# Integer intermediates, a fused product-and-maximum pass and PSUM-resident tiles in the feed-forward block of a Perceiver kernel

## What is computed

```python
def act_qdq(x):
    qmax = 2.0 ** (ACT_BITS - 1) - 1.0                  # 32767
    scale = jnp.maximum(jnp.max(jnp.abs(x)) / qmax, 1e-12)
    return jnp.clip(jnp.round(x / scale), -qmax - 1.0, qmax) * scale
def fixed_qdq_u16(x):
    scale = 1.0 / 65536.0
    return jnp.clip(jnp.round(x / scale), 0.0, 65535.0) * scale
x = act_qdq(x)
up = act_qdq(x @ lpbq_dequant(w_up).T)
gate = act_qdq(x @ lpbq_dequant(w_gate).T)
sig = fixed_qdq_u16(jax.nn.sigmoid(gate))
gate = act_qdq(gate * sig)
o = act_qdq(gate * up)
return o @ lpbq_dequant(w_down).T
```

## Time and profile before

| | us |
|---|---|
| Median of 3 runs (lowest, highest) | 1110.4 (1108.04, 1111.61) |
| Profiled execution, its own time | 1106.35 |
| Its span, first to last instruction | 1104.6 |
| TensorE busy in the span | 1025.6 (93%) |
| VectorE busy | 821.7 (74%) |
| ScalarE busy | 495.0 (45%) |
| GpSimd busy | 405.3 (37%) |

### The profile page before, as it was taken

The page is one execution under the profiler, slowest core; times in us unless marked ns, Lnnn a source line. Parts: engine busy times, 40 slices in busy tenths (PEclk is TensorE's granted clock), DMA queues, the critical chain, the costliest instruction groups (busy, mean ns, idle before and its releaser), DMA issues.

```text
span 1104.6 us, 14650 instructions
## 1 busy us (share of the span) xinstructions
PE 1025.6 (93%) x4907; PEld 481.3 (44%) x4907; DVE 821.7 (74%) x1186; ACT 495.0 (45%) x739; POOL 405.3 (37%) x218
## 2 busy tenths in 40 slices
PE   7999999999999989999839999999988889888997
PEld 3444444444444444544314444444452234465453
DVE  5566666799999558585974479999957777476897
ACT  2255555566666627415774211101036725356164
POOL 4287787400000363100002086776426740084003
PEclk9999999999999999999959999999999999999999
DMA  6146454623434056402010235435310020000001
GB/s 233 66 154 192 157 183 161 218 95 111 170 142 144 17 211 247 173 3 94 1 44 33 98 136 211 177 154 210 80 39 1 1 79 1 1 2 1 2 1 39
DMA packets 41831, 112.65 MB, mean 102 GB/s; under 512 B 4512, under 2 KB 15296, under 8 KB 35648
## 3 DMA queue, kind: packets, MB, share of 16 engines
q1 hardware_dynamic: 38592, 101.13, 26.1%
q10 hardware_dynamic: 2880, 9.96, 2.7%
q0 software_dynamic: 320, 1.05, 0.3%
HBM read 103.18 MB, written 7.34 MB: 100 GB/s over the span
## 4 chain that ended last, share of the span: by engine, by line
PE 69%; DVE 18%; ACT 5%; issue 3%; DMA 3%; POOL 1%; DVEq 0%; SPq 0%; ACTq 0%; POOLq 0%
PE PS L767 5%; PE PS L768 5%; PE PS L769 5%; PE PS L798 5%; PE PS L800 5%; PE PS L799 5%; PE PS L1709 5%; PE PS L1711 5%; PE PS L1710 5%; PE PS L249 3%; PE PS L251 3%; PE PS L250 3%; DVE arena L2087 2%; DMA arena<-in_w 2%; DVE arena L1632 2%
## 5 line engine op out<-in xcount | busy, mean ns | idle before, releaser
L798 PE MATMUL PS<-arena 128*128 128x512 f16 x256 | 97.0, 379 | 2.4 <-DVE arena L689 1.3
L767 PE MATMUL PS<-arena 128*128 128x512 f16 x256 | 97.0, 379 | 2.0 <-DVE arena L616 2.0
L1709 PE MATMUL PS<-arena 128*128 128x512 f16 x256 | 97.0, 379 | 1.8 <-DVE arena L1555 1.8
L768 PE MATMUL PS<-arena 128*128 128x512 f16 x256 | 97.0, 379 | 0.0
L769 PE MATMUL PS<-arena 128*128 128x512 f16 x256 | 97.0, 379 | 0.0
L1710 PE MATMUL PS<-arena 128*128 128x512 f16 x256 | 97.0, 379 | 0.0
L1711 PE MATMUL PS<-arena 128*128 128x512 f16 x256 | 97.0, 379 | 0.0
L800 PE MATMUL PS<-arena 128*128 128x512 f16 x256 | 97.0, 379 | 0.0
L799 PE MATMUL PS<-arena 128*128 128x512 f16 x256 | 97.0, 379 | 0.0
L623 DVE TENSOR_TENSOR arena<-PS,arena 128x512 f32<-128x512 f32 x64 | 43.6, 681 | 58.0 <-ACT arena L547 58.0
L481 POOL TENSOR_TENSOR arena<-arena 128x2048 f16<-128x2048 f32 x16 | 66.0, 4127 | 38.4 <-ACT arena L540 38.1
(11 more groups left out here) (381 smaller groups left out, 2437.1 us busy)
## 6 DMA issues: line engine op xcount, KB each, us to landing
arena<-in_ctxT SPq DMA_DIRECT2D x32, 1024.0 KB, 6.2
arena<-in_ctx SPq DMA_DIRECT2D x16, 1024.0 KB, 5.3
arena<-in_w ACTq DMA_DIRECT2D x8, 1024.0 KB, 5.4
arena<-in_w SPq DMA_DIRECT2D x8, 1024.0 KB, 6.6
XN<-in_ffnGU SPq DMA_DIRECT2D x16, 384.0 KB, 3.4
XN<-in_WinT SPq DMA_DIRECT2D x16, 290.0 KB, 5.0
gu_hi<-arena SPq DMA_DIRECT2D x16, 192.0 KB, 3.5
gu_lo<-arena SPq DMA_DIRECT2D x16, 192.0 KB, 3.4
```

The costliest lines, as they stand in the source:

```text
L767: pe.matmul(bank, CHI[:, b, e, cols], QHI[:, e, :], start=(e == 0), stop=False)
L768: pe.matmul(bank, CHI[:, b, e, cols], QLO[:, e, :], start=False, stop=False)
L798: pe.matmul(PS[:, t, :], PHI[:, j, cols], CHI[:, b, j, :], start=False, stop=False)
L1709: pe.matmul(bank, QHI3[:, e, cols], CHI3[:, b, e, :], start=(e == 0), stop=False)
```

## The change

Six things are changed, all in stage 2.

1. GpSimd rounds the gate. Between its second and third maximum it now makes, for each slice, `GT * RC + ROUND` in place (pass 1) and `GT - ROUND` as 16-bit integers into `GQ` (pass 2). ScalarE takes the magnitude of the rounded slice as integers (`GABS`) behind pass 1 and the sigmoid behind pass 2.
2. VectorE makes the 16-bit sigmoid integer in one pass (`SGQ`), without ScalarE's rounding pass. Then one `tensor_tensor_reduce` multiplies `GABS` by `SGQ` and keeps the maximum; the product itself (`JUNK`) is not used.
3. The scale of the gated gate now comes before that of up (scale 2 and 3 change places). Behind it VectorE makes the gated integers for all slices (`gated_int`), ScalarE their magnitudes (`gated_abs`).
4. ScalarE copies only six of the twelve up tiles (`COPIED`); VectorE reduces the other six straight from PSUM, and ScalarE reads them there.
5. Behind the scale of up ScalarE makes the magnitudes `UABS` of six slices and then the integers `UQ` of six slices; VectorE makes the second maximum with `tensor_tensor_reduce` again. The slices that lie in the banks of the down projection go first (`U_ORDER`).
6. Behind the last scale VectorE makes the hidden integer tile by tile, ScalarE casts it to `HID_HI`, VectorE subtracts for `HID_LO`.

The core of the diff, with ScalarE's and VectorE's removed functions left out:

```diff
-        SG = view(48 * K, [F0T, N])
+        SG = view(48 * K, [2, 1024])
+        JUNK = view(56 * K, [2, 1024], BF16)
+        SGQ = view(60 * K, [F0T, N], U16)
+        GQ = view(160 * K, [F0T, N], I16)
+        GABS = view(172 * K, [2, 1024], I16)
+        HALVES = view(24 * K, [F0T // 2, 2, 1024], I16)
+        UABS = view(60 * K, [F0T, N], I16)
+        UQ = view(160 * K, [F0T, N], I16)
...
+            reduce_all(1)
+            pool.wait_ge(s2_scale, 2)
+            for k in range(SLICES):
+                pool.tensor_scalar(flat(GT, k), flat(GT, k), RC[:, 1:2], ROUND, ALU.mult,
+                                   ALU.add).then_inc(s2_gate_q, 1)
+                pool.wait_ge(s2_gate_q, 2 * k + 1)
+                pool.tensor_scalar(flat(GQ, k), flat(GT, k), ROUND, None, ALU.subtract).then_inc(s2_gate_q, 1)
+            for n in range(2, 5):
+                reduce_all(n)
...
             for k in range(SLICES):
+                gate_magnitude(k)
                 gate_sigmoid(k)
+                take_up(k)
+
+            for k in range(SLICES):
+                act.wait_ge(s2_gated, SLICES + k + 1)
+                act.activation(gated_abs(k), gated_int(k), ACT.Abs).then_inc(s2_sig, 1)
+
             act.wait_ge(s2_scale, 4)
+            for k in U_ORDER:
+                act.activation(flat(UABS, k), up_source(k), ACT.Abs, scale=RC[:, 3:4]).then_inc(s2_up, 1)
+            for k in U_ORDER:
+                act.activation(flat(UQ, k), up_source(k), ACT.Copy, scale=RC[:, 3:4]).then_inc(s2_up, 1)
+            for i, g in enumerate(HID_ORDER):
+                act.wait_ge(s2_prod, i + 1)
+                act.copy(HID_HI[:, g, :], hidden_int(g)).then_inc(s2_gt, 1)
...
+            for k in range(SLICES):
+                dve.wait_ge(s2_sig, 2 * k + 2)
+                dve.tensor_scalar(flat(SGQ, k), SG[:, k % 2, :], 65536.0, 65535.0, ALU.mult,
+                                  ALU.min).then_inc(s2_gated, 1)
+                dve.wait_ge(s2_gated, k + 1)
+                if k >= 2:
+                    dve.wait_ge(s2_tmag, gated_taken(k - 2))
+                dve.tensor_tensor_reduce(JUNK[:, k % 2, :], GABS[:, k % 2, :], flat(SGQ, k), 1.0, 0.0, ALU.mult, ALU.max,
+                                         TILE_MAG[:, 0, k:k + 1]).then_inc(s2_tmag, 1)
+                if k < SLICES - 1:
+                    up_magnitude(k)
...
+            scale_of(2, unit=GUNIT)
+            dve.wait_ge(s2_scale, 3)
+            for k in range(SLICES):
+                dve.scalar_tensor_tensor(out=gated_int(k), in0=flat(GQ, k), scalar=RC[:, 2:3], in1=flat(SGQ, k),
+                                         op0=ALU.mult, op1=ALU.mult).then_inc(s2_gated, 1)
+                if k % 2:
+                    up_magnitude(SLICES + k // 2)
+            for g in range(SLICES + SLICES // 2, F0T):
+                up_magnitude(g)
...
-            pe.wait_ge(s2_tmag, NT + 2 * F0T + 2 * SLICES - 1)
+            pe.wait_ge(s2_tmag, NT + 2 * F0T + 2 * SLICES - 2)
             fill(pe, 0, 20)
+            pe.wait_ge(s2_up, COPIED + SLICES + 2)
```

More of the change, by code:

```diff
@@ L22 @@
 I16 = mybir.dt.int16
+U16 = mybir.dt.uint16
 I32 = mybir.dt.int32
@@ L1093, in take_up @@
                 act.wait_ge(s2_up_psum, g + 1)
[L1094 to L1105 removed]
+                act.copy(UP[:, g, :], PS[:, (F0T + g) % 8, :]).then_inc(s2_up, 1)
@@ L1202, in s2_dve @@
             scale_of(1)
-            def gate_whole(k):
-                dve.wait_ge(s2_gt_r, k + 1)
-                dve.tensor_scalar(tiles(GT, k), tiles(GT, k), ROUND, None, ALU.subtract).then_inc(s2_gt_q, 1)
-            def gated(k, between=None):
-                dve.wait_ge(s2_sg_r, k + 1)
-                link(dve.tensor_scalar(tiles(SG, k), tiles(SG, k), ROUND, 65535.0, ALU.subtract, ALU.min))
-                if between is not None:
-                    between()
-                link(dve.scalar_tensor_tensor(out=tiles(GT, k), in0=tiles(SG, k), scalar=1.0 / 65536.0, in1=tiles(GT, k),
-                                              op0=ALU.mult, op1=ALU.mult))
-                dve.tensor_reduce(TILE_MAG[:, 0, k:k + 1], tiles(GT, k), AX.XY, ALU.max,
-                                  apply_absolute_value=True).then_inc(s2_tmag, 1)
@@ L1257, in s2_dve, with product @@
             scale_of(4, unit=SCP)
-            link(dve.tensor_scalar(HUNIT, SC[:, 4:5], 1.0 / W_UP, None, ALU.mult))
-            for g in range(F0T):
-                dve.wait_ge(s2_sg_r, SLICES + g + 1)
-                dve.scalar_tensor_tensor(out=HID_LO[:, g, :], in0=GT[:, g, :], scalar=ROUND, in1=HID_HI[:, g, :],
-                                         op0=ALU.subtract, op1=ALU.subtract).then_inc(s2_hid, 1)
+            dve.wait_ge(s2_scale, 5)
+            link.note(dve.tensor_scalar(HUNIT, SC[:, 4:5], 1.0 / W_UP, None, ALU.mult))
+            def product(i):
+                g = HID_ORDER[i]
+                dve.wait_ge(s2_up, COPIED + SLICES + i // PER + 1)
+                half = slice((g % PER) * N, (g % PER + 1) * N)
+                dve.scalar_tensor_tensor(out=hidden_int(g), in0=UQ[:, g, :], scalar=RC[:, 4:5],
+                                         in1=gated_int(g // PER)[:, half],
+                                         op0=ALU.mult, op1=ALU.mult).then_inc(s2_prod, 1)
+            product(0)
+            for i, g in enumerate(HID_ORDER):
+                if i + 1 < F0T:
+                    product(i + 1)
+                dve.wait_ge(s2_gt, F0T + i + 1)
+                dve.tensor_tensor(HID_LO[:, g, :], hidden_int(g), HID_HI[:, g, :], ALU.subtract).then_inc(s2_hid, 1)
+            link.wait()
             for t in range(NT):
```

147 lines of the change are left out of this document (67 added, 80 removed).

## The result

The changed kernel takes 1116.54 us (median of 5 runs, 1114.38 to 1119.68) against 1110.4 before (1108.04 to 1112.61): a ratio of 1.0061, 95% interval 1.0042 to 1.0080. That is 6.1 us slower, where +0.2 was forecast: slower by over 0.3%, inside the range, and not the way that was forecast.

A forecast was written before the change was run, and what follows sets the result against it. Stage 2's relay from the gate's maximum (520.35) to the down projection's first matmul was taken as the bound; loads, passes and hand-overs put that matmul at 578.7 against 578.48, +0.2, so 1110.6 us, range 1103.0 to 1117.0.

The forecast's parts named there:

- The first load, 7.0: Change of GpSimd's code behind the gate's maximum, before its first rounding pass: 7.0 us, bounds 0 to 9.15.
- GpSimd's passes, 13.9 plus 4.6 of turns: GpSimd's twelve gate-rounding passes: 13.9 us with gaps, plus 4.6 waiting for VectorE; done at 545.9.
- The turns: GpSimd and VectorE alternate in the gate's stretch; four casts and four products cost GpSimd 4.6 us. Rival without turns: 0.08.
- VectorE's tail, 5.0: VectorE's last casts, products, magnitude and reduction behind GpSimd's last pass: 5.0 us, to 550.9.
- The second load, 5.8: GpSimd's code change ahead of the gated gate's maximum: 5.8 us, ending at 551.7, 0.8 later than VectorE.
- The product pass at 1.22: VectorE's product-and-maximum pass: 1.22 us, bounds 0.69 and 2.44, plus 0.19 for reading the result.
- The rival of half rate: VectorE's product-and-maximum pass runs at 2.44 us: +13.0 us, 1123.4; chance 0.10.
- Gated integers to the scale of up, 10.4, 0.3 and 1.1: VectorE's six multiplications and six PSUM reductions 10.4, last reduction and hand-over 0.3, maximum with scale 1.1: to 564.6.
- From there to the matmul, 14.1: Scale of up to first down-projection matmul: ScalarE's twelve passes 12.6, then cast, subtraction, hand-overs; 14.1 us, to 578.7.
- Feeding the down projection, nothing: In the down projection VectorE's two passes a tile, 1.4 against TensorE's 2.6, cost no time.
- forecast relay of 58.35: Stage 2 waits from the end of the gate's maximum, 520.35, to the down projection's first matmul, 578.7; previously 58.1 us.
- loads at 8.9 us: Rival: both GpSimd loads cost about 8.9 us, adding 1.9 and 3.1: +5.2 us, 1115.6; chance 0.19.

The follow-up runs named there:

- e3: Changed kernel with GpSimd's second pass written as times 1.0, plus -ROUND, in place of a lone subtract: median 1111.19 us, ratio 1.0013 to before.
- e2_no_pool: Changed kernel with the gate's rounding taken from GpSimd: VectorE makes the integers, ScalarE's magnitude reads the unrounded gate; median 1099.42 us, ratio 0.9888 to before.
- e9_scalar_touch: e2_no_pool plus one GpSimd tensor_scalar over a single unused column between the last two maxima: median 1102.80 us, ratio 0.9926 to before.
- e4_bench: e2_no_pool plus eight GpSimd passes over a scratch slice of 1024 columns, in idle time ahead of the gate's maximum: 1099.26 us (1 run).

## Why the prediction was wrong

Its steps, in order, each against the trace of the changed kernel:

- **The first load, 7.0: right.** 6.68 from the maximum's end (521.46) to GpSimd's first pass (528.14); in all runs with it 6.7 to 7.5 us. The Trainium skill's figure ("GPSIMD Engine Reference", Instruction dispatch), about 6 us with 5.95 measured, is below all of these; the case agrees with it that no instruction is seen.
- **GpSimd's passes, 13.9 plus 4.6 of turns: here it failed.** The sentence was "A pass by a constant over 1024 columns is 1.05". The row is one of a multiplication and an addition, the change's pass a lone subtraction, and that took 2.78: 10.4 us more in six. I had priced an instruction by its engine, shape and number of inputs, and not by its operations. A nearer row was at hand: in its last stage the kernel before takes the same constant off on GpSimd as a pair, times 1.0 plus -ROUND (L2323), in 0.62 us for 512 columns. The turns, on the other hand, did not come: beside the slow passes VectorE's product stayed at 1.22, and only its cast grew, to 1.50 to 1.56 in five of six. Together 23.8 us (528.14 to 551.95) for 18.5: +5.3. I gave this term no bounds either, though the trace had no lone operation of GpSimd.
- **VectorE's tail, 5.0: became irrelevant.** With GpSimd that slow VectorE keeps up, and needs 3.4 behind the last pass (551.95 to 555.34).
- **The second load, 5.8: right.** 5.91, and it ends last, as forecast. 5.8 to 6.1 in the other runs.
- **The product pass at 1.22: right**, 1.225 over SBUF integers. The rival of half rate is out. The rule of the Trainium skill beside it ("Vector Engine (DVE) Microarchitecture Reference", Points that are easy to get wrong) did not show here: two non-bf16 SBUF sources and an accumulator, and no halving; but the profile lists the pass as a custom instruction, and whether the rule means that form is not shown. Reading the accumulator showed as 0.08, not 0.19.
- **Gated integers to the scale of up, 10.4, 0.3 and 1.1: nearly right.** 11.15 and 0.96 (558.97, 570.12, 571.08).
- **From there to the matmul, 14.1: nearly right.** 13.46 (571.08 to 584.54), by ScalarE's twelve passes as forecast; the dummy matmuls were over at 583.35.
- **Feeding the down projection, nothing: right.** 31.1 us from the first matmul to the end in both kernels (578.48 to 609.56, 584.54 to 615.62), though two VectorE passes took 2.37 and 4.29 beside GpSimd's.

The sum of the differences: -0.3 + 5.3 + 0.1 + 0.45 - 0.15 - 0.65 = +4.75, which takes the forecast relay of 58.35 to the 63.1 measured. With the one edit of e3 the relay was 57.9 and the median 1111.19, so no second error of that size hides behind the first. That GpSimd's 18.5 came out to the tenth in e3 is partly luck: two slices without turns came every 2.22 us, which makes 13.3 for six in place of 13.9, and the four with turns took 1.3 more each in place of 1.15.

The rival nearest in time, loads at 8.9 us (1115.6), gave almost the measured number by the wrong cause: the loads were 6.7 and 5.9. A time alone would have confirmed it.

Seen whole, the change is worth about 11 us without GpSimd (e2_no_pool, 1099.42 against some 1111). The two loads and twelve passes on GpSimd turn this into a loss of 6, 17.2 us of relay in all; the loads are 8.8 of these, by the two "issue" rows of the first chain above (6.30 and 2.52).

## What to carry over

Price an instruction by a row of the same engine and the same operations, and if there is none, give the term bounds: on GpSimd two ways to write the same subtraction differed by 2.7 times. Before work is moved to GpSimd on a relay, look at what stands around it on its list: a tensor_scalar between two maxima over partitions cost some 13 us of GpSimd's time in two loads, for one column as for twelve passes, and what of it reached the end was what no idle time or other queue covered (8.8 us in the changed kernel, 3.3 in e9_scalar_touch). And when a step is made shorter, look for what is late next; the casts brought forward gained nothing until the dummy matmuls were cut.

## What was not expected of the hardware

- One-input passes of GpSimd over 1024 f32 columns: "times, plus" 1.04 to 1.05 us, to int16 and to f32; lone subtraction or addition 2.77 to 2.81; cast to int16 2.43; lone multiplication 3.82 and "subtract, plus 0.0" 3.64. VectorE ran passes of two inputs beside most of the slow ones, so the last two figures may not be the plain price. VectorE wrote int16 from f32 in 0.69.
- A GpSimd memset between two maxima needed no load (0.16 us), a tensor_scalar of one column two (7.46 and 6.06 us). A load is made as soon as GpSimd's list comes to it, without waiting for the data: behind idle time the maximum started 0.2 us after VectorE's result.
- GpSimd's fast passes and VectorE's passes with two inputs slow each other (1.05 to 1.89, 1.23 to 2.02); GpSimd's slow passes and the same VectorE passes did not (2.77 and 1.22). A two-input pass over 1536 f32 columns on VectorE did grow beside a slow pass (1.75 to 2.35 in e4_bench), and the slow pass did not (2.81).
